# Accumulating transfers, PSUM sums and ScalarE block copies in a Mamba-and-FFN kernel

## The chip, the cores and the metric

The kernel runs on one core of one Trainium2 chip. The metric is the device time of one launch in microseconds (us), the median of three runs. TensorE is called PE, VectorE DVE, ScalarE ACT, GpSimd POOL; SyncE (SP) only issues transfers here.

## What is computed

The reference, cut to what matters: one row sequence of 4096 tokens with 1024 features goes through a selective-scan block and then through a linear layer with dequantised weights, both with a layer norm ahead and a residual behind.

```python
proj = layernorm(x) @ in_proj_w                       # 1024 -> 2 * 2048
x1, z = split(proj)
xc = silu(causal_conv(x1, width 4) + conv_b)          # per channel
ssm_p = xc @ x_proj_w.T                               # 2048 -> 64 + 16 + 16
dt_r, Bm, Cm = rmsnorm of the three parts of ssm_p
dt = softplus(dt_r @ dt_proj_w.T + dt_bias)           # 64 -> 2048
h_t = exp(dt_t * A) * h_(t-1) + dt_t * B_t * xc_t     # state: 2048 channels x 16
ys_t = sum over the 16 states of h_t * C_t
y = (ys + D * xc) * silu(z)
x = x + y @ out_proj_w.T                              # 2048 -> 1024
x = x + layernorm(x) @ W.T + bias                     # 1024 -> 1024, W dequantised
```

All of it is float32.

## The kernel before

**Chunks and steps.** The 4096 tokens are taken in 16 chunks of T = 256, the 2048 channels in 8 pairs of 128-channel tiles. The main part is 16 iterations (`c`) of 8 steps (`j`), 128 steps S = 8c + j, all written out. Step S does the scan of pair j of chunk c and, beside it, a piece of four other stages: the input projection of x for pair S + 9, of z and dt for S + 1, the small projection to dt, B and C (`pair_proj`) for S + 8, column block j of the out projection of chunk c - 1 (from c = 1 on) and column block j of the FFN of chunk c - 2 (from c = 2 on; its matmuls run at the start of the step after). "First" and "last" below are steps j = 0 and j = 7 of a chunk. They carry more: the first the transposes and ScalarE work of the second layer norm, the last those of the first layer norm and the root mean squares of dt, B and C. Nothing is scheduled by a tool: each engine runs its instructions in the order written, and semaphores hold it back.

**The scan.** A step has 16 units u of two states each, four units to a PSUM ring `hb0` to `hb3`. For a unit ACT saves the old state and writes two exponentials into the bank (`unit`, lines 1079 and 1083), DVE scans in place (line 1378) and multiplies by C into `hc` (`times_c`, line 1326); ACT may reuse a bank once the product of four units earlier is done. POOL makes the inputs `dbx` for two units at a time (`group_of_b`, line 486, 8 groups k of 4 states each a step, two buffers) and adds the halves of each group of `hc` into `half` (`group_sum`, line 494, 8 a step). PE adds each of these to `ys0` or `ys1` with two matmuls by the identity (`group_sum` of PE, line 574). After four groups DVE multiplies by the gate into `ybuf` (`y_gate`, line 1337): that of the second half stands in the next step, behind `product(1)` (`late_y`).

**Residual rows.** `x2` holds the rows of two chunks, 1 MB each, by parity of the chunk. Chunk c - 1 has its input loaded there in the first step of iteration c, and that buffer held chunk c - 3: so SP first waits for the last FFN block of c - 3, stores its rows to `out` (line 360), waits until that has landed, and loads the new rows (line 363). DVE adds an out-projection block from the PSUM bank `g1` onto these rows late in each step (`add_out`, behind `product(12)`), an FFN block early in the next (`add_ffn`, behind `product(0)`; both line 1304), and the small projection from `ys1` onto `ssm` (`pair_ss`, lines 1282 and 1285). POOL adds the bias to the rows in four parts a chunk (`add_bias`, line 504). `g1` is used by turns: FFN matmuls, DVE's add, out projection, DVE's add.

**Order on PE in a plain step** (neither first nor last): FFN block, late sums 6 and 7, half the out projection, `x_proj`, sum 0, half of x's input projection, sum 1, its other half, sums 2 and 3, dt, the other half of the out projection, half of z's, sum 4, the other half, sum 5.

## Time and profile before

| what | value |
|---|---|
| median of three runs | 4658.65 us (4651.46 to 4660.2) |
| the profiled execution, its own time | 4652.27 us |
| its span, first to last instruction | 4650.4 us |
| main part, 128 steps | from about 117 us to about 4515 us |
| a plain step from c = 2 on | 33.2 us |
| a whole chunk from c = 2 on | about 275.4 us |
| mean granted TensorE clock | 0.98 of full speed |

The profile is one execution, 1.9 us longer than its span, and 0.14% under the median. Busy shares of the four engines lie close together, so that the page's totals do not say who sets the pace: this is read from the stretches of single steps. One step is counted from one gate activation of ACT (line 1092) to the next, since this occurs once in a step.

### The profile page before, as it was taken

The page shows a single profiled execution, that of the slowest core. Times are in us where ns is not written, and L with a number is a line of the kernel's source. Part 1 is how long each engine was busy: PE and PEld are TensorE (multiplying, and loading weights), DVE is VectorE, ACT ScalarE, POOL GpSimd, SP SyncE. Part 2 cuts the span into 40 slices and gives each one's busy share as a digit, 9 for nine tenths or more (in the row PEclk, how much of TensorE's full clock was granted, in tenths as well). Part 3 has the DMA queues.
Part 4 walks back from the last instruction along what each step waited for, and adds up shares of the span by engine and source line. Part 5 has one row for each costly group of instructions (what it writes and reads, how often), then busy time and mean ns, then how long its engine had stood idle before and what let it go on. Part 6 is the DMA issues. An engine that isn't in the chain of part 4 may idle for free.

```text
span 4650.4 us, 80289 instructions
## 1 busy us (share of the span) xinstructions
PE 4425.4 (95%) x26656; PEld 4020.1 (86%) x26656; DVE 4164.3 (90%) x5745; ACT 3537.7 (76%) x8848; POOL 4034.5 (87%) x2942
## 2 busy tenths in 40 slices
PE   7788999999999999999999999999999999998879
PEld 6577889989898998989899898998989899897769
DVE  3899999999999999999999899999999999999871
ACT  3787787877878787787878878787887878777650
POOL 0898989989899998989899899999989999899870
PEclk9889999999999999999999999999999999999889
DMA  7324344353544435353444535335353443533232
GB/s 252 135 82 160 104 156 147 121 184 129 184 137 159 147 129 179 137 181 128 150 156 137 186 122 184 128 131 191 120 184 129 175 144 115 184 129 135 96 106 84
DMA packets 160286, 678.57 MB, mean 146 GB/s; under 512 B 21120, under 2 KB 30080, under 8 KB 110720
## 3 DMA queue, kind: packets, MB, share of 16 engines
q1 hardware_dynamic: 141440, 639.88, 39.6%
q10 hardware_dynamic: 18432, 33.56, 1.9%
q8 instruction: 212, 3.47, 0.3%
q14 instruction: 202, 1.65, 0.1%
HBM read 618.32 MB, written 55.05 MB: 145 GB/s over the span
## 4 chain that ended last, share of the span: by engine, by line
PE 65%; DVE 14%; POOL 8%; issue 7%; DMA 3%; ACT 2%; SPq 1%; POOLq 0%; DVEq 0%; ACTq 0%
PE gx L594 15%; PE ys L574 13%; PE g L767 12%; PE ys L614 12%; DVE hb L1378 9%; PE g L689 6%; POOL dbx L486 5%; DVE hc L1326 3%; POOL half L494 2%; PE ys L604 2%; PE ys L624 2%; PE hb L875 1%; DVE gx L1270 1%; DMA b_scratch<-ssmT 1%; DMA ybuf<-in_wf_scales 1%
## 5 line engine op out<-in xcount | busy, mean ns | idle before, releaser
L1378 DVE TENSOR_TENSOR_SCAN hb<-hb,dbx 128x512 f32<-128x512 f32 x2048 | 2496.7, 1219 | 110.8 <-ACT hb L1083 77.2
L486 POOL TENSOR_TENSOR dbx<-dtx,bb 128x1024 f32<-128x1024 f32 x1024 | 2421.2, 2364 | 68.9 <-DVE hb L1378 43.9
L1083 ACT ACTIVATE hb<-dt,a_neg 128x256 f32<-128x256 f32 x4096 | 1789.3, 468 | 66.3
L494 POOL TENSOR_TENSOR half<-hc 128x512 f32<-128x512 f32 x1024 | 1305.3, 1275 | 86.0 <-DVE hc L1326 85.1
L1326 DVE TENSOR_TENSOR hc<-hb,cb 128x512 f32<-128x512 f32 x2048 | 1376.2, 672 | 0.0
L574 PE MATMUL ys<-half,ident 128*128 128x256 f32 x4096 | 1057.2, 390 | 115.4 <-POOL half L494 99.1
L574 PEld LDWEIGHTS ys<-half,ident 128*128 128x128 f32 x4096 | 764.1, 194 | 242.9 <-POOL half L494 131.4
L767 PEld LDWEIGHTS g<-wo,ybuf 128*128 128x128 f32 x7680 | 909.3, 194 | 27.5 <-issue 15.2
L614 PE MATMUL ys<-xnT,wz 128*128 128x256 f32 x4096 | 931.5, 381 | 1.3 <-DVE ybuf L1337 1.3
L594 PE MATMUL gx<-xnT,wx 128*128 128x256 f32 x3968 | 903.6, 382 | 21.8 <-issue 11.0
L767 PE MATMUL g<-wo,ybuf 128*128 128x128 f32 x7680 | 915.0, 277 | 9.0 <-issue 9.0
L594 PEld LDWEIGHTS gx<-xnT,wx 128*128 128x128 f32 x3968 | 756.1, 191 | 131.5 <-issue 14.3
L614 PEld LDWEIGHTS ys<-xnT,wz 128*128 128x128 f32 x4096 | 773.2, 191 | 104.0 <-DVE ybuf L1337 2.1
L1079 ACT COPY hstate<-hb 128x2 f32<-128x2 f32 x2044 | 319.5, 156 | 703.2 <-DVE hc L1326 698.8
L689 PEld LDWEIGHTS g<-wf,x2nT 128*128 128x128 f32 x3552 | 414.1, 192 | 5.7
L689 PE MATMUL g<-wf,x2nT 128*128 128x128 f32 x3552 | 414.5, 275 | 0.0
L1270 DVE SCALAR_TENSOR_TENSOR gx<-xpre,convw,gx 128x256 f32<-128x256 f32 x744 | 301.9, 480 | 11.7 <-ACT gx L964 11.6
L1304 DVE TENSOR_TENSOR x<-g,x 128x256 f32<-128x256 f32 x240 | 99.8, 416 | 178.2 <-PE g L689 139.6
L512 POOL TENSOR_TENSOR dtx<-dt,xcs 128x2 f32<-128x2 f32 x128 | 25.3, 198 | 234.0 <-ACT dt L1014 227.8
L604 PE MATMUL ys<-xprojw,xcn 128*128 128x96 f32 x1024 | 140.7, 283 | 32.5 <-ACT xcn L973 23.8
L1089 ACT ACT_TABLE_LOAD x128 | 164.2, 1283 | 2.3
L1010 ACT ACT_TABLE_LOAD x128 | 164.2, 1283 | 2.3
(105 smaller groups left out, 2739.1 us busy)
## 6 DMA issues: line engine op xcount, KB each, us to landing
wz<-in_win SPq DMA_DIRECT2D x128, 1024.0 KB, 4.8
wx<-in_win SPq DMA_DIRECT2D x124, 1024.0 KB, 4.8
wo<-in_wout SPq DMA_DIRECT2D x123, 1024.0 KB, 5.0
wf<-wf_scratch SPq DMA_DIRECT2D x113, 512.0 KB, 3.9
xc_scratch<-xcn ACTq DMA_DIRECT2D x128, 256.0 KB, 3.7
xcs<-xc_scratch SPq DMA_DIRECT2D x128, 256.0 KB, 5.0
bb<-bc_scratch SPq DMA_DIRECT2D x64, 512.0 KB, 8.8
cb<-bc_scratch SPq DMA_DIRECT2D x64, 512.0 KB, 8.0
```

The source lines that it names most:

```text
L486: nc.gpsimd.tensor_tensor(dbx[:, k % 2, :].rearrange("p (n t) -> p n t", n=NQ), dtx[:, S % 2, a, :].unsqueeze(1).to_broadcast([P, NQ, T]), ...
L494: nc.gpsimd.tensor_tensor(half[:, k % 4, :], hc[:, k % 2, 0:HALF], hc[:, k % 2, HALF:GW], ALU.add).then_inc(halves, 1)
L574: mm = nc.tensor.matmul(ys[a][:, 0:T], ident[:], half[:, k % 4, i * T:(i + 1) * T], start=False, stop=(q == NQ - 1 and i == 1), skip_group ...
L594: mm = nc.tensor.matmul(pair_bank(q)[:, a * T:(a + 1) * T], pair_weights(q)[:, kk, a * P:(a + 1) * P], xnT[:, chunk % 2, kk, :], start=(kk ...
L614: mm = nc.tensor.matmul(ys[0][:, a * T:(a + 1) * T], wz[:, kk, a * P:(a + 1) * P], xnT[:, q // PAIRS % 2, kk, :], start=(kk == 0), stop=(k ...
L689: mm = nc.tensor.matmul(g1[:, tt * P:(tt + 1) * P], x2nT[:, kk, tt * P:(tt + 1) * P], wf[:, kk, :], start=(kk == 0), stop=(kk == KH - 1))
L767: mm = nc.tensor.matmul(g1[:, tt * P:(tt + 1) * P], ybuf[:, (1 - st.parity) * PAIRS + kt // 2, (kt % 2) * T + tt * P:(kt % 2) * T + (tt + ...
L1079: nc.scalar.copy(hstate[:, ds(2 * js * N + 2 * us, 2)], h[:, T - 1:UW:T]).then_inc(kept, 1)
L1083: ins = nc.scalar.activation(h[:, m * T:(m + 1) * T], dt[:, j % 2, a, :], ACT.Exp, scale=a_neg[:, ds((2 * j + a) * N + 2 * v + m, 1)])
L1270: nc.vector.scalar_tensor_tensor(bank[:, a * T:(a + 1) * T], xpre[:, a, tap:tap + T], convw[:, ds((2 * jq + a) * KC + tap, 1)], bank[:, a ...
L1326: nc.vector.tensor_tensor(hc[:, k % 2, w * UW:(w + 1) * UW], hb[u % 4][:], cb[:, n:n + 2, :].rearrange("p n t -> p (n t)"), ALU.mult).then ...
L1378: nc.vector.tensor_tensor_scan(h[:], h[:], dbx[:, k % 2, w * UW:(w + 1) * UW], 0.0, ALU.mult, ALU.add).then_inc(scans, 1)
```

## The change

- **Sums by a transfer.** Of the four groups of each half, the first two are now added by a transfer that POOL issues and that accumulates in SBUF (`add_group_pair`, 512 KB, twice a step); POOL adds the halves of the result (`pair_sum`). Six sums a step reach PE instead of eight, the order being groups 2 and 3 of the first half, its pair, group 2 of the second half, its pair, group 3. `half` has three places. PE's sums of the second half all move to the start of the next step.
- **Bias by a transfer.** One accumulating transfer of 1 MB a chunk instead of four POOL additions.
- **Blocks made onto their rows.** ACT copies a block of the rows into `g1` (`block_in`), PE's matmuls add onto it (`start=False`), and ACT copies it back (`block_out`). DVE's two adds a step are gone. ACT's copies stand behind unit 5 (FFN block out, out-projection block in) and at the step's end (out-projection block out, FFN block in).
- **dt, B and C** are summed over the eight pairs in the free columns of `g1`; ACT squares and copies the sum once a chunk and writes zeros. DVE's `pair_ss` is gone.
- **Order.** On PE `x_proj` and half of x's projection come ahead of the out projection, dt comes behind the first sum; on DVE `y_gate` of the first half comes two units later.
- SP's order of transfers is as before, but the store of the rows waits for `f_out`, which ACT's copy of the FFN block raises, where it waited for DVE's add.

The diff, cut to its core:

```diff
+        hd = sb("hd", [P, 3, GW])
         hc = sb("hc", [P, 2, GW])
-        half = sb("half", [P, 4, HALF])
+        half = sb("half", [P, PLACES, HALF])
...
                     if first and st.before(first).ffn:
-                        sp.wait_ge(f_add, after(PAIRS * (c - 2)))
+                        sp.wait_ge(f_out, after(PAIRS * (c - 2)))
                         sp.dma_start(out_rows[c - 3], x2_rows(1 - st.parity)).then_inc(out_st, 16)
...
+            def add_group_pair(S, a):
+                pool.wait_ge(hcs, after(UNITS * S + UNITS // 2 * a + 4))
+                pool.dma_start(hd[:, 2 * a, :], hd[:, 1, :], accum_op=ALU.add).then_inc(hd_acc, 16)
+            def pair_sum(S, a):
+                pool.wait_ge(hd_acc, 16 * (2 * S + a + 1))
+                nc.gpsimd.tensor_tensor(sum_place(SUMS * S + PAIR_SUM[a]), hd[:, 2 * a, 0:HALF],
+                                        hd[:, 2 * a, HALF:GW], ALU.add).then_inc(halves, 1)
...
+            def add_bias(chunk):
                 pool.wait_ge(l2_ready, after(2 * (chunk + 1)))
+                pool.dma_start(x2_rows(chunk % 2), ffn_bias.partition_broadcast(P).unsqueeze(1)
+                               .to_broadcast([P, TT, H]), accum_op=ALU.add).then_inc(bias_acc, 16)
...
+                    products(1)
+                    if not (first and c == 0):
+                        pair_sum(S - 1, 1)
+                        group_sum(S - 1, 1, 1)
+                    products(2)
+                    products(3)
+                    add_group_pair(S, 0)
+                    products(4)
+                    group_sum(S, 0, 0)
+                    products(5)
+                    group_sum(S, 0, 1)
+                    products(6)
+                    pair_sum(S, 0)
+                    if first and st.ffn:
+                        add_bias(c - 2)
+                    products(7)
+                    add_group_pair(S, 1)
...
             def pair_proj(q):
                 pe.wait_ge(sx_act, after(q + 1))
+                if q % PAIRS == 0:
+                    pe.wait_ge(ssm_zero, after(q // PAIRS + 1))
-                        mm = nc.tensor.matmul(ys[1][:, tt * E:(tt + 1) * E],
+                        mm = nc.tensor.matmul(g1[:, T + tt * E:T + (tt + 1) * E],
...
                     def ffn():
-                        if was.outproj:
-                            g1_after_o()
+                        pe.wait_ge(f_pre, after(S - 2 * PAIRS))
...
                     def out_proj(part):
-                            if was.ffn:
-                                g1_after_f()
+                            pe.wait_ge(o_pre, after(S - PAIRS + 1))
...
+                    def blocks_between():
+                        if st.inproj:
+                            act.wait_ge(xp_mm, after(S + PAIRS + 1))
+                        if st.before(first).ffn:
+                            ffn_out(S)
+                        if last and st.inproj:
+                            chunk_square(c + 1)
+                        if st.outproj:
+                            act.wait_ge(xres_in, landed(c))
+                            act.wait_ge(f_out, after(S - 2 * PAIRS))
+                            block_in(c - 1, j, o_pre)
+                    def out_out():
+                            act.wait_ge(o_mm, after(S - PAIRS + 1))
+                            block_out(c - 1, j, o_out)
+                    def ffn_in():
+                            act.wait_ge(o_out, after(S - PAIRS + 1))
+                            act.wait_ge(bias_acc, 16 * (c - 1))
+                            block_in(c - 2, j, f_pre)
...
                     unit(5)
                     norm1(1)
+                    blocks_between()
                     unit(6)
...
                     unit(15)
+                    if not last:
+                        out_out()
+                    ffn_in()
...
                     product(0)
-                    add_ffn()
...
                     product(4)
-                    add_x_proj()
...
                     product(12)
-                    add_out()
```

The order on PE from the start of a plain step, before. L689 is the FFN block, L574 a sum, L767 the out projection, L604 `x_proj`, L594 x's input projection.

```order
L689 MATMUL g<-wf,x2nT 128x128 [waits o_add,l2_evac,wf_in]
L689 MATMUL g<-wf,x2nT 128x128 x15
L574 MATMUL ys<-half,ident 128x256 [waits halves]
L574 MATMUL ys<-half,ident 128x256
L574 MATMUL ys<-half,ident 128x256 [waits halves]
L574 MATMUL ys<-half,ident 128x256
L767 MATMUL g<-wo,ybuf 128x128 [waits f_add,wo_in]
L767 MATMUL g<-wo,ybuf 128x128 x15
L604 MATMUL ys<-xprojw,xcn 128x96 [waits sx_act,y_ready]
L604 MATMUL ys<-xprojw,xcn 128x96 x3
```

The same place in the changed kernel (L721 FFN, L610 a sum, L642 `x_proj`, L630 x's projection, L794 the out projection).

```order
L610 MATMUL ys<-half,ident 128x256 [waits halves]
L610 MATMUL ys<-half,ident 128x256
L642 MATMUL g<-xprojw,xcn 128x96 [waits sx_act]
L642 MATMUL g<-xprojw,xcn 128x96 x3
L630 MATMUL gx<-xnT,wx 128x256 [waits sx_act,l1_evac,wx_in]
L630 MATMUL gx<-xnT,wx 128x256 x7
L794 MATMUL g<-wo,ybuf 128x128 [waits o_pre,wo_in]
L794 MATMUL g<-wo,ybuf 128x128 x7
```

The out projection now waits for ACT's copy (`o_pre`) with `x_proj` and half of x's projection ahead of it; in a first step x's projection is not ahead, so only `x_proj` is.

The order on ACT around unit 5 of a first step, before. L1079 and L1083 are a unit, L1102 the skip term, L931 a row of the second norm.

```order
L1102 ACTIVATE ys<-xcs,dparam 128x256 [waits xc_in0,sz_act]
L1079 COPY hstate<-hb 128x2 [waits hcs]
L1083 ACTIVATE hb<-dt,a_neg 128x256 [waits kept]
L1083 ACTIVATE hb<-dt,a_neg 128x256
L1079 COPY hstate<-hb 128x2 [waits hcs]
L1083 ACTIVATE hb<-dt,a_neg 128x256 [waits kept]
L1083 ACTIVATE hb<-dt,a_neg 128x256
L931 ACTIVATE xrow<-x,nmr,rstd 128x1024 [waits l1_tr]
```

And in the changed kernel (L1158 the skip term, L1135 and L1139 a unit, L1028 `block_out`, L1024 `block_in`).

```order
L1158 ACTIVATE ys<-xcs,dparam 128x256 [waits xc_in0,sz_act]
L1135 COPY hstate<-hb 128x2 [waits hcs]
L1139 ACTIVATE hb<-dt,a_neg 128x256 [waits kept]
L1139 ACTIVATE hb<-dt,a_neg 128x256
L1028 COPY x<-g 128x2x128 [waits f_mm,xp_mm]
L1024 COPY g<-x 128x256 [waits f_out,xres_in]
L1135 COPY hstate<-hb 128x2 [waits hcs]
L1139 ACTIVATE hb<-dt,a_neg 128x256 [waits kept]
L1139 ACTIVATE hb<-dt,a_neg 128x256
L954 ACTIVATE xrow<-x,nmr,rstd 128x1024 [waits l1_tr]
```

Two copies stand between units 5 and 6; the second waits for the loaded rows (`xres_in`).

The order on SP at the same place, in the changed kernel: the last transfer of a chunk and the next four.

```order
L409 DMA wz<-in_win 128x2048 [waits z_mm]
L372 DMA out<-x 128x2x1024 [waits f_out]
L375 DMA x<-in_x 128x2x1024 [waits out_st]
L380 DMA xcs<-xc_scratch 128x512 [waits dtx_ready,dx1]
L384 DMA wf<-wf_scratch 128x1024 [waits f_mm,wf_st]
```

No transfer moved; the store waits for `f_out`, the load for the store.

## Rows read from the trace of the kernel before

**Rows 1.** The page's engine totals: busy us, share of the span, instructions.

```profile
PE 4425.4 (95%) x26656; PEld 4020.1 (86%) x26656; DVE 4164.3 (90%) x5745; ACT 3537.7 (76%) x8848; POOL 4034.5 (87%) x2942
```

**Rows 2.** Stretches: length, busy of PE, PEld, DVE, ACT, POOL, granted clock, DMA, GB/s.

```profile
2217.20:2250.40 33.20, 33.20 (x206) 30.61 (x205) 32.33 (x46) 25.90 (x65) 30.81 (x23) 1.00 0.38 130
2322.00:2357.40 35.40, 33.29 (x200) 29.71 (x201) 31.12 (x42) 30.02 (x72) 33.53 (x27) 1.00 0.69 254
2283.40:2322.00 38.60, 36.96 (x230) 33.23 (x228) 34.67 (x51) 31.27 (x86) 31.29 (x24) 1.00 0.47 162
2046.70:2322.10 275.40, 270.70 (x1666) 247.89 (x1664) 259.06 (x359) 220.52 (x554) 251.99 (x183) 1.00 0.44 151
396.50:669.40 272.90, 251.97 (x1395) 224.20 (x1396) 256.84 (x352) 216.56 (x548) 247.63 (x181) 0.96 0.38 136
4243.00:4484.00 241.00, 201.93 (x1141) 176.44 (x1140) 205.42 (x254) 170.81 (x420) 219.28 (x159) 0.89 0.28 98
```

**Rows 3.** Chain that ended last, within one plain step: start us, us, what.

```profile
2217.39 1.73 PE ys L574 x8
2219.11 3.57 PE g L767 x32
2222.68 0.87 PE ys L604 x8
...
2224.44 3.45 PE gx L594 x16
```

**Rows 4.** DVE's groups in that plain step: busy us, mean ns, idle before.

```profile
L1304 DVE TENSOR_TENSOR x<-g,x 128x256 f32<-128x256 f32 x2 | 0.8, 416 | 1.0 <-PE g L689 1.0
...
L1285 DVE TENSOR_TENSOR ssm<-ys,ssm 128x192 f32<-128x192 f32 x1 | 0.3, 341 | 0.0
```

**Rows 5.** POOL's and ACT's groups by shape, over the whole span.

```profile
L486 POOL TENSOR_TENSOR dbx<-dtx,bb 128x1024 f32<-128x1024 f32 x1024 | 2421.2, 2364 | 68.9 <-DVE hb L1378 43.9 <-POOL bb L464 0.4
...
L494 POOL TENSOR_TENSOR half<-hc 128x512 f32<-128x512 f32 x1024 | 1305.3, 1275 | 86.0 <-DVE hc L1326 85.1
...
L1102 ACT ACTIVATE ys<-xcs,dparam 128x256 f32<-128x256 f32 x256 | 117.1, 457 | 0.0
```

**Rows 6.** Timeline of a plain step's start: start us, us, engine, instruction, idle before.

```profile
2212.98 1.22 DVE L1378 TENSOR_TENSOR_SCAN hb<-hb,dbx 128x512 f32<-128x512 f32 x1
...
2214.81 0.16 ACT L1079 COPY hstate<-hb 128x2 f32<-128x2 f32 x1 [0.65 <-DVE hc L1326]
...
2217.68 0.59 ACT L973 ACTIVATE xcn<-gx 128x512 f32<-128x512 f32 x1
...
2221.18 0.87 ACT L1083 ACTIVATE hb<-dt,a_neg 128x256 f32<-128x256 f32 x2
```

**Rows 7.** SP's timeline where a chunk ends: the store and the load.

```profile
2321.31 0.39 SPq L360 DMA_DIRECT2D out<-x  x1
2331.97 0.38 SPq L363 DMA_DIRECT2D x<-in_x  x1
```

**Rows 8.** Transfers by tile: times issued, KB each, median us to landing.

```profile
wf<-wf_scratch SPq DMA_DIRECT2D x113, 512.0 KB, 3.9
...
bb<-bc_scratch SPq DMA_DIRECT2D x64, 512.0 KB, 8.8
...
x<-in_x SPq DMA_DIRECT2D x16, 1024.0 KB, 5.0
out<-x SPq DMA_DIRECT2D x14, 1024.0 KB, 11.5
```

**Rows 9.** The store of line 360 alone, 13 of them.

```profile
DMA to landing us min/median/max: 6.5/11.5/11.9
```

**Rows 10.** Timeline in the last chunk: PE after it stood still.

```profile
4499.51 2.08 PE L574 MATMUL ys<-half,ident 128*128 128x256 f32 x4 [2.70 <-POOL half L494]
...
4504.91 5.29 PE L767 MATMUL g<-wo,ybuf 128*128 128x128 f32 x32
```

**Rows 11.** Issue of a transfer by SP where a queue is full: start us, us.

```profile
2332.45 1.84 SPq L368 DMA_DIRECT2D xcs<-xc_scratch  x1
```

More of the change, by code:

```diff
@@ L412, in store_columns @@
                 h = slice(half * H // 2, (half + 1) * H // 2)
-                sp.wait_ge(f_add, after(PAIRS * chunk + (half + 1) * PAIRS // 2))
+                sp.wait_ge(f_add, after(PAIRS * (chunk - NC + 2) + (half + 1) * PAIRS // 2))
                 sp.dma_start(out_rows[chunk][:, :, h], x2_rows(chunk % 2)[:, :, h]).then_inc(out_st, 16)
@@ L560, in _, with group_sum @@
             iterations(iteration)
-            group_sum(NC * PAIRS - 1, 7)
+            pair_sum(NC * PAIRS - 1, 1)
+            group_sum(NC * PAIRS - 1, 1, 1)
             for chunk in (NC - 2, NC - 1):
-                for i in range(4):
-                    add_bias(chunk, i)
+                add_bias(chunk)
         @block.tensor
         def _(pe):
-            def group_sum(SG, k):
-                a, q = divmod(k, NQ)
-                pe.wait_ge(halves, after(8 * SG + k + 1))
-                for i in range(2):
-                    mm = nc.tensor.matmul(ys[a][:, 0:T], ident[:], half[:, k % 4, i * T:(i + 1) * T],
-                                          start=False, stop=(q == NQ - 1 and i == 1), skip_group_check=True)
+            def group_sum(SG, i):
+                n = SUMS * SG + i
+                pe.wait_ge(halves, after(n + 1))
+                for w in range(2):
+                    mm = nc.tensor.matmul(ys[i // 3][:, 0:T], ident[:], half[:, n % PLACES, w * T:(w + 1) * T],
+                                          start=False, stop=(i % 3 == 2 and w == 1), skip_group_check=True)
                 mm.then_inc(sum_mm, 1)
@@ L634, in _ @@
             pe.wait_ge(id_ready, after(1))
+            for m in range(4):
+                mm = nc.tensor.matmul(g1[:, m * P:(m + 1) * P], ident[:], ident[:], start=(m == 0), stop=True,
+                                      skip_group_check=True)
+            mm.then_inc(g1_marked, 1)
             pe.wait_ge(l1_ready, after(2))
@@ L689, in ffn, with late_groups @@
                                 mm = nc.tensor.matmul(g1[:, tt * P:(tt + 1) * P], x2nT[:, kk, tt * P:(tt + 1) * P],
[L690 removed]
+                                                      wf[:, kk, :], start=False, stop=(kk == KH - 1),
+                                                      skip_group_check=True)
                         mm.then_inc(f_mm, 1)
[L693 removed]
+                    def late_groups():
                         if was.scan and not (first and c == 0):
[L695 removed]
+                            pe.wait_ge(dx1, after(S))
+                            for k in range(3, SUMS):
+                                group_sum(S - 1, k)
                     def group(k):
@@ L709, in x_proj @@
                         if st.inproj:
-                            if was.scan and not (first and c == 0):
-                                pe.wait_ge(y_ready, after(2 * S))
-                            else:
-                                pe.wait_ge(xp_add, after(S + PAIRS))
+                            if was.outproj and not was.ffn:
+                                pe.wait_ge(o_out, after(S - PAIRS))
                             pair_proj(S + PAIRS)
@@ L882, in _ @@
             pe.wait_ge(wf_in, landed(LAST - 2 * PAIRS))
-            pe.wait_ge(o_add, after(LAST - PAIRS))
+            pe.wait_ge(f_pre, after(LAST - 2 * PAIRS))
             for tt in range(TT):
@@ L886, in _ @@
                     mm = nc.tensor.matmul(g1[:, tt * P:(tt + 1) * P], x2nT[:, kk, tt * P:(tt + 1) * P],
-                                          wf[:, kk, :], start=(kk == 0), stop=(kk == KH - 1))
+                                          wf[:, kk, :], start=False, stop=(kk == KH - 1), skip_group_check=True)
             mm.then_inc(f_mm, 1)
-            group_sum(LAST - 1, 6)
+            pe.wait_ge(dx1, after(LAST))
+            for k in range(3, SUMS - 1):
+                group_sum(LAST - 1, k)
             pe.wait_ge(l2_ready, after(2 * (NC - 1)))
@@ L1465, in step @@
                     product(9)
-                    if not (last and st.norm1):
-                        y_gate(S, 0)
                     scan(11)
@@ L1471, in step @@
                     product(11)
-                    if last and st.norm1:
-                        y_gate(S, 0)
+                    y_gate(S, 0)
                     if not edge:
@@ L1493, in last_ffn @@
             def last_ffn(chunk, j):
-                dve.wait_ge(bias_add, after(4 * chunk + j // 2 + 1))
+                dve.wait_ge(bias_acc, 16 * (chunk + 1))
                 dve.wait_ge(f_mm, after(chunk * PAIRS + j + 1))
```

224 lines of the change are left out of this document (100 added, 124 removed).

## The prediction

> **What bounds the kernel now.** The page's totals come first: PE 95%, DVE 90%, POOL 87%, ACT 76% busy [rows 1]. They name no single bound, so the second view is the table by stretches. In a plain step of 33.2 us PE is busy for all of it, DVE for 32.33 us, POOL for 30.81, ACT for 25.9; over a whole chunk of 275.4 us PE is busy for 270.7 [rows 2]. The third view, the chain within such a step, holds nothing but PE's pieces one behind the other [rows 3]. So PE sets the pace from chunk 2 on, with DVE about 1 us a step behind it: its one idle time is the 1.0 us in which it waits for the FFN block [rows 4]. Where less falls to PE, in iteration c = 1 (no FFN), the chunk still takes 272.9 us with DVE at 256.84 [rows 2]: take PE away and DVE is next, at 94% of the time.
>
> **What PE loses.** Eight sums are 1.73 us a pair: 0.87 us each, two matmuls of two passes [rows 3]. Two go, so the plain step's PE work falls from 33.2 to 31.5 us, and the chunk's from 270.7 by 8 x 1.73 to 256.9.
>
> **What DVE loses.** Two adds of 0.416 us and one of 0.341 [rows 4], 1.17 us: 32.33 - 1.17 = 31.2 us of work. It is no longer held by the FFN block itself, but `late_y` still stands behind it, since all three sums of the second half come after that block.
>
> **What POOL loses and gets.** Two sums of 1.275 us a step [rows 5] and four bias additions a chunk of about the same go: 30.81 - 2.55 = 28.3 us or less. Two transfers a step come, plus one a chunk, and POOL is held while it issues them. No row shows POOL issuing a transfer. SP's issues take from 0.38 us [rows 7] to 1.84 us where a queue was full [rows 11], and POOL's longest instruction over the same 128x1024 tile takes 2.36 us [rows 5]. I take 1.3 us, near the middle, close to what POOL needs for half such a tile: 28.3 + 2.6 = 30.9 us, under PE's 31.5. From 1.6 us on POOL would set the pace, and at 2.36 us it would stand at 33.0, the step's length now.
>
> The Trainium skill (DMA: Bandwidth & Descriptors, SWDGE vs HWDGE vs iDMA and Latency and other measured facts) says that an accumulating transfer must come from GpSimd, whose cores write the descriptors, and puts the first byte at about 1 us; by that figure, an estimate, POOL's step would be 30.3 us, and nothing in the sum would move.
>
> **Landing.** The first transfer of a step is issued about 10 us after scan 0 and wanted by POOL about 20 us after it; the second is issued at about 24.5 and wanted at about 34.5. The window is some 9 us. Rows of 512 KB landed in 3.9 us (`wf`) and 8.8 us (`bb`, several at once) [rows 8]. An accumulating one also reads its target, so I take 6 us, hidden; the upper row just fits.
>
> **What ACT gets.** Four copies of 128x256 a step, priced by its skip term into PSUM, 0.457 us [rows 5]: 1.8 us. ACT was busy for 25.9 of 33.2 us, so there is room, but its copies are now in PE's chain. Let D be the start of scan 0 (2212.98). ACT starts unit 3 at D + 1.8, has the silu done at D + 5.3 and unit 5 at D + 9.1 [rows 6]; two copies later, at about D + 10.1, the rows are in `g1` (`o_pre`). PE meanwhile has the FFN block, three sums, `x_proj` and half of x's projection: about up to D + 10. From there to the end of the next step's late sums it has 27.1 us (4 x 1.79 out projection, 3 x 3.45 x and z, 6 x 0.87 sums, dt, FFN 3.57 [rows 3]), so `late_y` comes at D + 37.9 where DVE alone would reach it at D + 31.1 + 5.2 = D + 36.3. This asks PE and DVE to settle a little above 31.5; I take **31.9 us** for the plain step, 1.3 less than now.
>
> **The first step of a chunk, where the change costs.** Before, the last FFN block was added at the step's start, the rows stored at once (2321.31), the load issued 10.7 us later (2331.97) [rows 7], landed about 5.0 us after that [rows 8]; all this was hidden, because the loaded rows were wanted only by `add_out` behind `product(12)`, about 30 us into the step. Now the FFN block is copied out behind unit 5, and the very next instruction on ACT waits for the load that follows the store that follows this copy. Nothing covers it. In a first step ACT also has the start of the second norm (some 1.2 us), so the block is out at about D + 10.8. Store: 13 of them landed in 6.5 to 11.9 us, median 11.5 [rows 9], where they shared the engines with the chunk's B and C and z's weights (DMA share 0.69 [rows 2]). Now it starts 10 us later, when those have landed, so I take 6.5; load 5.0 [rows 8]; issue and copy 0.9. So `o_pre` comes at D + 23.2. Behind it on ACT's queue are all of units 6 to 15, so DVE and POOL stop too after a unit or two, and PE, which has only `x_proj` ahead of it in this step, stands from about D + 7.5, 15.7 us. After `o_pre` it has 7.2 out projection, 4 x 3.45 x and z, 6 x 0.87 sums, 0.87 dt, 1.8 transposes and 3.57 FFN, 32.4 us, up to the late sums of the next step: D + 55.6. In the settled loop these end 5.9 us into a step, so the next step begins at D + 49.7. PE that had stood still ran four passes in 2.08 us and the out projection's half in 5.29 where it takes 3.57 [rows 10, 3], with a granted clock of 0.89 in that chunk [rows 2]: 2 us more. **First step 52 us** in place of 35.4 [rows 2].
>
> The Trainium skill (DMA: Bandwidth & Descriptors, Anatomy of one DMA) gives a transfer 2.0 us plus its bytes over 436 GB/s, so an estimate of 4.4 us for 1 MB each way. The trace disagrees for both: 5.0 us for the load, never under 6.5 us for the store [rows 8, 9]. By the page the pair would take 8.8 us instead of 11.5, and the sum below would fall by 13 x 2.7 = 35 us.
>
> **The sum.** Last step: 38.6 us [rows 2], less 1.3 as the others, less 1.0 because dt now runs ahead of two sums: 36.3. A chunk: 52 + 36.3 + 6 x 31.9 = 279.7 us against 275.4, +4.3, times 12 for c = 3 to 14: +52. Iteration c = 2 has no store, so its first step is about 38.3 us and the chunk 266: -9.5. c = 1: DVE falls by 8 x 0.76 = 6.1 us of 256.84, and at the same share the chunk by 6.5. c = 0: -3. c = 15: PE is not its bound (201.93 of 241 us [rows 2]); 8 x 1.3 are saved, 12 lost to the store and load: +2. In the tail two transfers of 1 MB must land before the last FFN adds: +2. Together 52 - 9.5 - 6.5 - 3 + 2 + 2 = +37, say +40 to +45, since the waits I cannot see add time oftener than they take it. The profiled execution took 4652.3 us, 6 under the median: 4652 + 43 = 4695, and against the median about **4700 us**, 0.9% slower. The gain of some 1.3 us in 120 steps and a stall of 12 us and its aftermath in 13 steps nearly cancel.
>
> **Rivals.**
> 1. *The stall is shorter, faster than before.* If the rows are in `g1` 5 us earlier than I say in each first step (the store alone in 4 us, ACT early), 13 x 5 = 65 us go: 4635 us. For it: the store will be nearly alone. Against it: no store of 1 MB landed under 6.5 us. It becomes faster once store and load together take less than about 8 us. Chance 0.17 for under 4649.
> 2. *The store stays slow.* At the median of 11.5 us [rows 9] it adds 13 x 5 = 65 us: 4765. The first accumulating transfer of the step does start beside it. Chance 0.2.
> 3. *ACT's copies eat the gain.* If `o_pre` and `f_pre` hold PE so that the plain step stays at 33.2 us, about 100 steps lose 1.3 us: 4830. Chance 0.08.
> 4. *POOL's issue costs 2.4 us.* Then its step is 33.1 us of work and about 34.2 with its waits: 2.3 x 110 = 250 us more, 4950. Decides from 1.6 us. Chance 0.09.
> 5. *The accumulating transfer lands in 11 us*, over its window of 9: `pair_sum` holds POOL, the late sums and `late_y` by 2 us a step: 4900 or more. Chance 0.06.
>
> **How the numbers follow.** The forecast, 4650 to 4740, has 0.40. About 0.2% is what a measurement of this kernel can tell from no change, here 4649 to 4668: 0.1, from the forecast's lower end. Faster 0.17, slower 0.73. The range leaves out the lowest ends of rival 1 and rivals 4 and 5: 4625 to 4850.
>
> **What the profile after would show.** PE's sums 3072 passes instead of 4096; plain steps of about 31.9 us with PE still nearly full. In 13 first steps a wait of ACT of some 12 us on the load before a copy of `g1`, PE idle for 15 us before the out projection, SP's store and load issued back to back in the middle of the step's first half, and a lower granted clock behind it. POOL's issue near 1.3 us and no wait on `hd_acc`. The prediction is wrong if the wait for the rows is short, if plain steps are at 33 us or above, or if DVE waits for `dbx` in every step.

## The result: 3.1% slower

The changed kernel takes 4799.9 us (median of 4 runs, 4796.3 to 4805.0) against 4656.4 us beside it, a ratio of 1.031 with a 95% interval of 1.029 to 1.033: 143 us more, where some 43 were forecast. The sign and the stall in a chunk's first step were as forecast; the size was not, and most of what is missing lies in the last step of a chunk.

The page after, its totals and some of its costliest groups, answers to [rows 1, 4, 5]:

```profile
span 4803.2 us, 77941 instructions
...
PE 4304.4 (90%) x25640; PEld 3908.0 (81%) x25640; DVE 4054.7 (84%) x5385; ACT 3688.8 (77%) x9345; POOL 3887.9 (81%) x2894
...
L794 PE MATMUL g<-wo,ybuf 128*128 128x128 f32 x7680 | 1001.1, 288 | 207.5 <-ACT g L1024 207.5
...
L610 PE MATMUL ys<-half,ident 128*128 128x256 f32 x3072 | 808.4, 399 | 177.8 <-POOL half L516 103.7
...
L511 POOL DMA_DIRECT2D hd<-hd x256 | 225.8, 882 | 15.4 <-issue 2.9
L1024 ACT COPY g<-x 128x256 f32<-128x256 f32 x232 | 86.6, 373 | 164.1 <-DMA x<-in_x 139.3
```

PE, DVE and POOL have lost 121, 110 and 147 us of work, and the span has grown by 153. The 207.5 us that PE waits for ACT's copy of the rows (L1024, `block_in`) are the first thing to look at. The table by stretches (length, busy of PE, PEld, DVE, ACT, POOL, granted clock, DMA, GB/s) says where they lie: a plain step, the last step of a chunk, the first step and the second step of the next, and a whole chunk.

```profile
2500.90:2533.00 32.10, 31.69 (x197) 29.12 (x197) 31.11 (x42) 27.19 (x69) 30.04 (x23) 1.00 0.56 167
2629.80:2672.90 43.10, 36.76 (x214) 33.20 (x212) 32.62 (x47) 33.03 (x91) 28.68 (x23) 0.92 0.54 162
2672.90:2722.50 49.60, 36.17 (x208) 32.93 (x209) 31.90 (x41) 31.46 (x77) 33.60 (x27) 0.83 0.70 232
...
2672.90:2959.90 287.00, 264.93 (x1605) 242.25 (x1606) 252.54 (x336) 231.00 (x589) 244.41 (x182) 0.96 0.59 179
...
2722.50:2755.50 33.00, 32.55 (x202) 29.91 (x202) 31.18 (x42) 27.32 (x70) 30.11 (x23) 1.00 0.60 179
```

Steps are measured here and below from one silu of the gate to the next on ACT, as means over c = 3 to 13; the lines of a profile show single steps. The sum by steps:

| us | before | forecast | after |
|---|---|---|---|
| first step | 35.7 | 52 | 49.6 |
| second step | 34.9 | 31.9 | 33.0 |
| plain steps, five | 33.2 | 31.9 | 32.1 to 32.4 |
| last step | 38.5 | 36.3 | 43.1 |
| chunk | 275.2 | 279.7 | 287.0 |
| c = 2, first step | 36.5 | 38.3 | 44.5 |
| c = 2, chunk | 275.9 | 266 | 281.9 |

The forecast's chunk is 7.3 us too short, and the last step alone is 6.8 of it. The other errors (first -2.4, second +1.1, plain +1.8 in all) nearly cancel.

**The first step.** PE after the sums and `x_proj`; ACT; SP (start us, us, what, idle before):

```profile
2676.93 1.03 PE L642 MATMUL g<-xprojw,xcn 128*128 128x96 f32 x8
2689.75 7.45 PE L794 MATMUL g<-wo,ybuf 128*128 128x128 f32 x48 [11.79 <-ACT g L1024]
```
```profile
2678.00 0.37 ACT L1028 COPY x<-g 128x256 f32<-128x256 f32 x1 [0.21 <-PE g L642]
2689.23 0.38 ACT L1024 COPY g<-x 128x256 f32<-128x256 f32 x1 [10.86 <-DMA x<-in_x]
```
```profile
2678.40 0.39 SPq L372 DMA_DIRECT2D out<-x  x1
2683.89 0.38 SPq L375 DMA_DIRECT2D x<-in_x  x1
```

This is the forecast stall. The FFN block is out at 2678.37, the store is issued at 2678.40, the load 5.5 us later, and ACT goes on 5.3 us after that. PE stands for 11.8 us and then runs 48 passes of the out projection in 7.45 us, under a granted clock of 0.74 in that stretch and of 0.83 over the step. (A pass is what the trace counts: each float32 matmul of the kernel shows as two.) The Trainium skill (DMA: Bandwidth & Descriptors, Anatomy of one DMA) gives its 2.0 us plus bytes over 436 GB/s as a fit for transfers that GpSimd issues; taken for these two, which SP issues, it would make an estimate of 4.4 us each, and the trace has 5.5 and 5.3.

**The last step.** PE and ACT in the same stretch:

```profile
2632.14 0.60 PE L617 MATMUL gx<-ident,xrow 128*128 128x128 f32 x4
2634.22 0.66 PE L617 MATMUL gx<-ident,xrow 128*128 128x128 f32 x4 [1.48 <-ACT xnT L971]
2637.21 3.75 PE L794 MATMUL g<-wo,ybuf 128*128 128x128 f32 x16 [2.33 <-ACT g L1024]
2640.76 1.06 PE L617 MATMUL gx<-ident,xrow 128*128 128x128 f32 x4
```
```profile
2635.54 0.36 ACT L1028 COPY x<-g 128x256 f32<-128x256 f32 x1
...
2636.71 0.36 ACT L1024 COPY g<-x 128x256 f32<-128x256 f32 x1
...
2641.86 0.58 ACT L971 COPY xnT<-gx 128x512 f32<-128x512 f32 x1 [3.79 <-PE gx L617]
```

The norm transposes share one bank (`gx`), so between two of them PE waits for ACT's evacuation. Before, `x_proj` and a quarter of the out projection filled the first of these gaps. Now `x_proj` runs ahead of the transposes, and the out projection waits for `block_in`, which stands on ACT behind units 4 and 5, two evacuations and four small operations. PE stands for 1.5 and 2.3 us, runs the next 16 passes in 3.75 us at a granted clock of 0.50 (1.95 us where the clock is 1.00), and ACT, which wants the third transposes, waits 3.8 us for them. Which of these links carries the cost was settled only by experiment.

### The profile page after: what moved, and what is told of

Read it like the earlier page. It is cut to its first block, busy times and chain, and to the rows that moved or that the text cites. A ratio compares the mean times of both kernels' runs of the same rounds, so it can differ in the third digit from the quotient of the medians.

```text
span 4803.2 us, 77941 instructions
## 1 busy us (share of the span) xinstructions
PE 4304.4 (90%) x25640; PEld 3908.0 (81%) x25640; DVE 4054.7 (84%) x5385; ACT 3688.8 (77%) x9345; POOL 3887.9 (81%) x2894
## 3 DMA queue, kind: packets, MB, share of 16 engines
q1 hardware_dynamic: 141296, 639.35, 36.8%
## 4 chain that ended last, share of the span: by engine, by line
PE 48%; POOL 25%; issue 9%; DVE 8%; ACT 5%; DMA 5%; SPq 0%; POOLq 0%; ACTq 0%; DVEq 0%
POOL dbx L498 17%; PE ys L653 14%; PE ys L610 10%; PE g L794 9%; PE g L721 7%; DVE hb L1457 5%; PE gx L630 4%; POOL half L522 3%; POOL half L516 3%; ACT hb L1139 2%; POOL hd L511 2%; DMA x<-in_x 1%; DMA out<-x 1%; PE hb L896 1%; DVE gx L1353 1%
## 5 line engine op out<-in xcount | busy, mean ns | idle before, releaser
L1139 ACT ACTIVATE hb<-dt,a_neg 128x256 f32<-128x256 f32 x4096 | 1789.2, 468 | 66.4
L794 PE MATMUL g<-wo,ybuf 128*128 128x128 f32 x7680 | 1001.1, 288 | 207.5 <-ACT g L1024 207.5
L794 PEld LDWEIGHTS g<-wo,ybuf 128*128 128x128 f32 x7680 | 992.3, 204 | 236.9 <-issue 215.8
L610 PE MATMUL ys<-half,ident 128*128 128x256 f32 x3072 | 808.4, 399 | 177.8 <-POOL half L516 103.7
L630 PE MATMUL gx<-xnT,wx 128*128 128x256 f32 x3968 | 907.3, 382 | 23.3 <-issue 10.8
L653 PEld LDWEIGHTS ys<-xnT,wz 128*128 128x128 f32 x4096 | 779.6, 193 | 115.7 <-DVE ybuf L1421 11.8
L630 PEld LDWEIGHTS gx<-xnT,wx 128*128 128x128 f32 x3968 | 741.9, 192 | 123.1 <-issue 14.3
L610 PEld LDWEIGHTS ys<-half,ident 128*128 128x128 f32 x3072 | 572.1, 198 | 288.9 <-POOL half L516 134.6
L522 POOL TENSOR_TENSOR half<-hc 128x512 f32<-128x512 f32 x512 | 650.6, 1271 | 175.3 <-DVE hc L1410 175.0
L1410 DVE TENSOR_TENSOR hd<-hb,cb 128x512 f32<-128x512 f32 x1024 | 688.8, 673 | 0.0
L1410 DVE TENSOR_TENSOR hc<-hb,cb 128x512 f32<-128x512 f32 x1024 | 688.8, 673 | 0.0
L1135 ACT COPY hstate<-hb 128x2 f32<-128x2 f32 x2044 | 318.6, 156 | 476.7 <-DVE hc L1410 393.7
L721 PEld LDWEIGHTS g<-wf,x2nT 128*128 128x128 f32 x3552 | 414.1, 192 | 5.7
L721 PE MATMUL g<-wf,x2nT 128*128 128x128 f32 x3552 | 414.5, 275 | 0.0
L516 POOL TENSOR_TENSOR half<-hd 128x512 f32<-128x512 f32 x256 | 325.5, 1272 | 0.9 <-DMA hd<-hd 0.9
L1421 DVE TENSOR_TENSOR ybuf<-ys,gate 128x256 f32<-128x256 f32 x256 | 107.4, 420 | 235.7 <-PE ys L610 235.5
L511 POOL DMA_DIRECT2D hd<-hd x256 | 225.8, 882 | 15.4 <-issue 2.9
L1024 ACT COPY g<-x 128x256 f32<-128x256 f32 x232 | 86.6, 373 | 164.1 <-DMA x<-in_x 139.3
```

The lines of the kernel that those rows point to most:

```text
L516: nc.gpsimd.tensor_tensor(sum_place(SUMS * S + PAIR_SUM[a]), hd[:, 2 * a, 0:HALF], hd[:, 2 * a, HALF:GW], ALU.add).then_inc(halves, 1)
L522: nc.gpsimd.tensor_tensor(sum_place(SUMS * S + LATER_SUMS[a][i]), hc[:, i, 0:HALF], hc[:, i, HALF:GW], ALU.add).then_inc(halves, 1)
L610: mm = nc.tensor.matmul(ys[i // 3][:, 0:T], ident[:], half[:, n % PLACES, w * T:(w + 1) * T], start=False, stop=(i % 3 == 2 and w == 1), s ...
L630: mm = nc.tensor.matmul(pair_bank(q)[:, a * T:(a + 1) * T], pair_weights(q)[:, kk, a * P:(a + 1) * P], xnT[:, chunk % 2, kk, :], start=(kk ...
L653: mm = nc.tensor.matmul(ys[0][:, a * T:(a + 1) * T], wz[:, kk, a * P:(a + 1) * P], xnT[:, q // PAIRS % 2, kk, :], start=(kk == 0), stop=(k ...
L721: mm = nc.tensor.matmul(g1[:, tt * P:(tt + 1) * P], x2nT[:, kk, tt * P:(tt + 1) * P], wf[:, kk, :], start=False, stop=(kk == KH - 1), skip ...
```

## Experiments

**1. The order of transposes and out projection on PE.** First theory: ACT's wait for the transposes.

```
 # last step
 norm1(0); norm1(1)
+norm1(2)
 out_proj(0)
-norm1(2)
 out_proj(1)
 # first step
 out_proj(0); out_proj(1)
-out_proj(2); norm2(0); out_proj(3); norm2(1)
+norm2(0); out_proj(2); norm2(1); out_proj(3)
```

> The changed kernel with another order on TensorE in two places and nothing else: in a chunk's last step the third group of norm transposes stands ahead of out_proj's first quarter (it stood behind it), and in a chunk's first step the norm transposes stand after the second and third quarter of out_proj instead of after the third and fourth. Theory A: the last step lost because ScalarE waits 3.0 + 0.9 us there for transposes that queue behind an out_proj that itself waits for ScalarE's block_in, and the first step because the transposes stand behind 24 matmuls of out_proj at half clock (3.3 us). Then the last step falls from 43.2 to about 39.3 us, the first step by about 3 us (c=2 from 44.5 to 41.5), and the time by 15 x 3.9 + 14 x 3 = about 100 us, to 4700. Rival B: the last step is long because ScalarE has 2 to 3 us more work of its own in it (block copies, the copy of the sums, zeroing); the order changes nothing and the last step stays at 43, the time at 4795 to 4805.

Measured: 4793.4 us, 1.030 (1.029 to 1.032); last step 42.5, first 49.7. Nearly nothing. But the trace of its last step shows that the order only exchanged one wait for another: the fourth transposes now stand behind 32 passes that take 6.4 us.

```profile
ACT xnT L971 <- PE gx L617: 4.6, 1, 4.6
```

So for the last step this run did not decide; in the first step the transposes came 16 passes sooner and the step did not move, so they were not its bound.

**2. Store and load of the rows in halves**, columns 0 to 511 a few steps ahead.

```
-if first: wait f_out(last block of c-3); store rows c-3; wait; load rows c-1
+if first:  wait f_out(last block of c-3); store columns 512.. of c-3
+if j == 1: wait that store;               load  columns 512.. of c-1
+if j == 5: wait f_out(block 3 of c-2);    store columns ..511 of c-2
+if j == 6: wait that store;               load  columns ..511 of c
```

> The changed kernel with the store of the finished rows and the load of the next x rows into the same buffer cut into column halves: columns 0 to 511 are stored in step 5 of the chunk before and loaded in step 6, so that only columns 512 to 1023 move after the last ffn block is out, and out_proj's first block waits for neither. Theory A: the first step of c=3 to 15 is long because block_in waits for store and load in series (10.2 us on ScalarE, 13.4 us on TensorE), but part of that only hides other waits, which c=2's first step (44.5 us, no store in it) shows: 49.4 falls to 44.5, times 13 is 64 us, time 4736. Rival B: the stall is paid in full and nothing else is long there: 49.4 falls by 13.4 to 36, the first step of before, times 13 is 174 us, time 4626. Rival C: the moved transfers hold SyncE's queue in steps 5 and 6 (6.5 us store ahead of the load), later weights come late, and steps 5 to 7 take back 3 to 6 us a chunk: 4790 or more.

Measured: 4637.8 us, 0.9976 (0.9965 to 0.9987): 162 us less than the changed kernel. First steps fall from 49.6 to 38.0 us, and that of c = 2 from 44.5 to 37.5, so rival B came near (11.6 of 13.4 us a step) and theory A fell: c = 2 was no picture of a first step without the stall. It has no store, but its load is issued directly behind the B, C and z loads and takes 12.4 us, from 668.86 to the copy at 681.22, in the changed kernel:

```profile
668.38 0.43 SPq L409 DMA_DIRECT2D wz<-in_win  x1
668.86 0.43 SPq L375 DMA_DIRECT2D x<-in_x  x1
```
```profile
681.22 0.38 ACT L1024 COPY g<-x 128x256 f32<-128x256 f32 x1 [5.90 <-issue]
```

The trace of before has a like spread for its load (line 363, 15 of them):

```profile
DMA to landing us min/median/max: 4.8/5.0/12.6
```

The two long ones, 12.2 and 12.6 us, are those of c = 1 and c = 2, the chunks without a store; all others took 4.8 to 5.4.

The moved transfers cost nothing visible (rival C): plain and last steps stay at 32.1 to 32.4 and 42.7 us. The last step is hardly touched by it (43.1 to 42.7), so it is a loss of its own.

**3. The sums and the bias alone**, on the kernel before; blocks and `x_proj` sums stay with DVE. The places of PE's sums, of dt and of `y_gate` move with the sums, as in the change.

```
+hd[0..2]; add_group_pair (accumulating transfer), pair_sum, six sums a step
+add_bias by one accumulating transfer
 add_ffn(); add_out(); add_x_proj()   # as before, on DVE
```

> The kernel before with only two parts of the change: the first two groups of each half are added by an accumulating transfer (six sums on GpSimd and TensorE instead of eight), and the bias is added by one accumulating transfer. The out_proj and ffn blocks and the x_proj sums stay with VectorE's additions as before, in their old places, so there is no block_in and no stall behind the rows' store and load. Theory A: what the plain step won (33.2 to 32.2 us) is GpSimd's four sums less; it comes here too, first and last step stay as before (36 and 38.5 us), and the time is 4656 - 15 x (5 to 7 steps x 1.0 us) = 4550 to 4580. Rival B: it is VectorE's relief of three additions a step (VectorE is busy 94% of a chunk before), so the plain step stays at 33.2 and the time at 4645 to 4670. Rival C: transfer landing 5.6 us late delays the pair sum so that y_gate waits; with VectorE's additions behind it the step is longer than before: 4700 or more.

Measured: 4553.5 us, 0.979 (0.978 to 0.981). Theory A came true, and the kernel is faster than the one before and the changed one. The same stretches as above (plain, last, first, chunk):

```profile
2379.80:2412.10 32.30, 31.89 (x198) 29.12 (x197) 32.14 (x45) 26.00 (x66) 30.13 (x23) 1.00 0.56 165
2509.00:2545.70 36.70, 33.96 (x214) 30.33 (x212) 34.15 (x50) 31.21 (x86) 29.62 (x24) 1.00 0.62 185
2545.70:2581.50 35.80, 33.48 (x208) 29.85 (x209) 30.73 (x42) 29.99 (x71) 32.54 (x26) 1.00 0.99 325
2545.70:2813.30 267.60, 260.18 (x1603) 236.26 (x1604) 258.49 (x359) 220.17 (x554) 242.84 (x181) 1.00 0.63 192
```

The plain step is 32.3 us with DVE's three additions still in it, and on the mean of the five plain steps hardly less without (32.34 and 32.27): taking them from DVE is worth 0.1 us, the sums by transfer 0.9. How much of the 0.9 is PE's work, POOL's or the new places is not separated. The clock stays at 1.00.

**4. The complement**: the changed kernel with eight sums on POOL and PE.

```
-add_group_pair, pair_sum, six sums
+group_sum(S, 0..7), in before's places
```

> The complement: the changed kernel with the eight group sums on GpSimd and TensorE as before; blocks made onto their rows and left to ScalarE, the x_proj sums in PSUM and the bias transfer stay. Theory A (the win of the plain step is GpSimd's): the plain step goes back to 33.2 or more, a chunk to 286.8 + 6 to 8 us, the time to 4890 to 4920. Rival B (the win is VectorE's relief): plain step 32.2, time 4790 to 4810, as the changed kernel.

Measured: 4927.5 us, 1.060 (1.058 to 1.061). Plain step 33.5, chunk 296.7 (9.7 more than the changed kernel's), last step 43.8, first 49.8. So the blocks on ACT bring the long first and last steps by themselves, and win nothing in between. Only in c = 15, where PE has no in-projection, is it other: from its second step on its steps take 31.1 to 31.4 us here, 33.1 to 34.8 in the changed kernel, 32.1 to 36.1 before. There the blocks on ACT did shorten the step, and the transfers lengthened it beside them; without the blocks they did not (31.3 to 33.7 in run 3). Why is open.

**5, 6. All four transposes ahead of the out projection**, with the rows in halves; and with `out_out` behind unit 15.

```
 norm1(0); norm1(1)
+norm1(2); norm1(3)
 out_proj(0); out_proj(1)
 # and in 6, on ACT
-if last: out_out()      # ahead of unit(14)
 unit(14); x_taps(); unit(15)
-if not last: out_out()
+out_out()
```

> The split-rows kernel (4637.8 us; last step 43.2 us) with TensorE's order in a chunk's last step changed: all four groups of norm transposes stand ahead of out_proj's first quarter. The norms-first kernel had only exchanged the third group for a wait of 4.6 us for the fourth, behind 32 matmuls of out_proj (6.4 us at half clock), so it decided nothing. Theory A (ScalarE is held by transposes that queue behind out_proj): ScalarE's wait falls to under 1.5 us, the last step from 43.2 to 39.5, times 14 is 50 us, time 4588. Rival B (ScalarE's own added work, and VectorE and TensorE waiting for it, is what lengthens the step): out_proj starts 2 to 3 us later instead, the step stays at 42 to 43.5, time 4620 to 4645.

> As norms4_split, and in the last step the out_proj block is copied back after ScalarE's unit 15, as in all other steps, not between second_skip_term and unit 14, where ScalarE stands 1.5 us for out_proj's last quarter. Theory A: that wait is on the path of the exps that VectorE waits for: the last step is another 1.5 us shorter than norms4_split's, 14 x 1.5 = 21 us. Rival B: the copy is then late for the next ffn block, TensorE waits at the start of the next chunk, and the time is that of norms4_split or up to 15 us more.

Measured: 4629.1 us, 0.994 (0.993 to 0.996), last step 42.4; and 4634.4 us, 0.996 (0.994 to 0.997), last step 42.3. Theory A falls, this time cleanly: ACT's wait for the fourth transposes is down to 0.24 us and the step has not moved. PE has taken the wait over (4.1 us for evacuations), and ACT waits later, for the dt projection:

```profile
2547.95 1.11 PE L632 MATMUL gx<-ident,xrow 128*128 128x128 f32 x4 [1.83 <-ACT xnT L986]
```
```profile
2549.10 0.59 ACT L986 COPY xnT<-gx 128x512 f32<-128x512 f32 x1 [0.24 <-PE gx L632]
...
2562.72 0.17 ACT L1082 ACTIVATE dt<-ys 128x2 f32<-128x2 f32 x1 [2.45 <-PE ys L678]
```

What both orders leave as it was is that PE has nothing to run in the gaps. That gave the theory of run 9.

**7. The bias alone**, on the kernel before.

```
-add_bias(c - 2, 0..3): four additions on POOL
+add_bias(c - 2): one accumulating transfer
```

> The kernel before with only the bias changed: one accumulating transfer of 1 MB a chunk in the first step instead of four additions of 1.27 us on GpSimd. Theory A: GpSimd is not the bound of a plain step before (30.7 of 33.2 us, TensorE 33.2 of 33.2), the additions were hidden, so what the sums-and-bias kernel won (96 us) is all the sums': 4640 to 4655 here. Rival B: the transfer, landing after some 10 us beside the first step's loads, delays those: first step 36 to 38, time 4660 to 4680. Rival C: the bias additions held the step: 4600 to 4635.

Measured: 4656.9 us, 1.000 (0.999 to 1.001); chunk 275.3. No difference, so the 96 us that run 3 won beside its own runs of before come with the sums.

**8. The second transfer of a step issued 5.8 us later**, behind the small operations and the next step's first products, on run 3's kernel.

```
 products(7)
-add_group_pair(S, 1)
 inflow_of(S + 1); carry_of(S + 1); group_of_b(S + 1, 0, ...)
+add_group_pair(S, 1)
```

> The sums-and-bias kernel (4553.5 us) with the second accumulating transfer of a step issued after GpSimd's small operations (inflow, carry, the next step's first products) and not ahead of them. Theory A: the small operations are long (inflow 0.52 us for 0.24, carried 0.50 for 0.26, dtx 1.59 for 1.27) because the issue of the transfer is still going on behind them; issued later they go back to their times of before. In a plain step TensorE is busy 31.9 of 32.3 us, so the time hardly moves: 4540 to 4555. Rival B: those durations stay, they belong to another neighbour (VectorE's or the transfers' traffic); and the pair sum, 4 us later, comes too late for the late groups: 4560 to 4590.

Measured: 4751.9 us, 1.021 (1.019 to 1.022): 198 us more than run 3. Half of theory A holds: the small operations are back at 0.29 (inflow), 0.30 (carried) and 1.32 us (dtx), and the sum now behind the issue is long in some steps (median 1.31 us, up to 1.62, for 1.27). Its forecast of the time failed, and rival B's was far too low: POOL waits 124 times for the landing, in all 172.5 us; in run 3 that wait was 0.3 us in all, in the changed kernel 0.9.

```profile
L507 POOL TENSOR_TENSOR half<-hd 128x512 f32<-128x512 f32 x256 | 325.1, 1270 | 173.0 <-DMA hd<-hd 172.5
```

The issue in a plain step of run 3, from the products ahead of it to the pair's sum (L507):

```profile
2397.33 2.37 POOL L489 TENSOR_TENSOR dbx<-dtx,bb 128x1024 f32<-128x1024 f32 x1
2399.64 0.81 POOL L502 DMA_DIRECT2D hd<-hd  x1
...
2409.82 1.27 POOL L507 TENSOR_TENSOR half<-hd 128x512 f32<-128x512 f32 x1
```

And in run 8:

```profile
2515.14 2.37 POOL L489 TENSOR_TENSOR dbx<-dtx,bb 128x1024 f32<-128x1024 f32 x1
2517.46 0.21 POOL L528 TENSOR_TENSOR dtx<-dt,xcs 128x2 f32<-128x2 f32 x1
2517.61 1.27 POOL L532 TENSOR_TENSOR dtx<-dt,xcs 128x510 f32<-128x510 f32 x1
2518.84 0.24 POOL L542 TENSOR_TENSOR inflow<-dtx,b 128x32 f32<-128x32 f32 x1
...
2523.23 0.89 POOL L502 DMA_DIRECT2D hd<-hd  x1
...
2528.30 1.27 POOL L507 TENSOR_TENSOR half<-hd 128x512 f32<-128x512 f32 x1 [0.55 <-DMA hd<-hd]
```

From issue to sum POOL had 10.2 us, now 4.5 and the wait; the transfer took 5.0.

Plain steps grow by 0.7 us only, first steps from 36.3 to 43.6: there the landing is late beside the B and C loads. The waits of one such step (in all, times, longest):

```profile
DVE ybuf L1369 <- PE ys L601: 9.0, 2, 7.5
...
PE ys L601 <- POOL half L507: 6.6, 1, 6.6
...
POOL half L507 <- DMA hd<-hd: 4.2, 1, 4.2
```

**9, 10. ACT's block copies early in the last step**, with the rows in halves and with the changed kernel's own store and load.

```
 silus()
+if last: blocks_between()
 unit(4); first_skip_term(); norm1(0); unit(5); norm1(1)
-blocks_between()
+if not last: blocks_between()
 # PE, last step
 norm1(0)
+out_proj(0)
 norm1(1)
-out_proj(0)
 norm1(2); out_proj(1); norm1(3)
```

> The split-rows kernel (4637.8 us, last step 43.2 us) with ScalarE's block copies and the copy and zeroing of the sums put directly behind the silus in a chunk's last step (they stood behind unit 5 and the second norm evacuation), and on TensorE out_proj's first quarter directly behind the first norm transposes, as before the change. Theory A, formed after the two order kernels failed: TensorE has nothing to do between the norm transposes because out_proj is held by block_in until ScalarE has done units 4 and 5 and two evacuations; it stands 4.6 us there (1.5 + 0.8 + 2.3) and then runs at half clock, which makes 32 out_proj matmuls 6.4 us instead of 3.7. With block_in some 3 us earlier out_proj fills those gaps: granted clock of the last step from 0.92 to 0.98 or more, last step from 43.2 to 37.5 to 38.5, times 14 is 70 us, time 4560 to 4575. Rival B: ScalarE is simply short of time in this step (33 of 43 us busy, in pieces that VectorE waits for); units 4 and 5 come 1.6 us later now, VectorE waits for them, and the step stays at 42 to 43: 4625 to 4640.

> The changed kernel with ScalarE's block copies early in a chunk's last step as in blocks_early_split, but with the rows' store and load whole and in series as the change has them. If the two losses are separate, each is worth the same alone as beside the other: blocks_early_split was 50 us under split_rows, so this is 4800 - 50 = 4750, and the two together (162 + 50 us under the changed kernel's 4800) make the 4588 measured. If the stall at the chunk's start hides what the last step loses (the transfers' start depends on a block that ScalarE copies in the first step, so everything before it shifts alike), no such hiding is expected; were it there, the time would be 4790 to 4805.

Measured: 4587.6 us, 0.986 (0.984 to 0.987), last step 39.0; and 4754.6 us, 1.021 (1.020 to 1.023), last step 39.2. The last step of run 9, and PE at its start:

```profile
2521.80:2560.80 39.00, 34.08 (x214) 30.67 (x212) 33.20 (x47) 33.03 (x93) 29.34 (x23) 1.00 0.60 179
```
```profile
2524.19 0.60 PE L632 MATMUL gx<-ident,xrow 128*128 128x128 f32 x4
2526.07 2.02 PE L809 MATMUL g<-wo,ybuf 128*128 128x128 f32 x16 [1.28 <-ACT g L1039]
2527.93 0.61 PE L632 MATMUL gx<-ident,xrow 128*128 128x128 f32 x4
2529.37 0.66 PE L632 MATMUL gx<-ident,xrow 128*128 128x128 f32 x4 [0.82 <-ACT xnT L986]
```

The same matmuls and the same copies; PE's waits ahead of the third transposes are one of 1.3 us and one of 0.8 in place of 1.5 and 2.3, the 16 passes take 2.02 us, not 3.75, PE's busy time falls from 36.7 to 34.1 us and the granted clock rises from 0.92 to 1.00. Theory A holds as a mechanism, though the step (39.0 us) and the time (4588) stop short of its ranges, 37.5 to 38.5 and 4560 to 4575. The edit moves ACT's copies and PE's quarter together; runs 1 and 5 had moved PE's order alone to little effect (0.6 and 0.3 us off the last step). Rival B falls for these 3.7 us: ACT is busy for 33.0 us as before, and the step is shorter. The two losses nearly add: run 2 gave back 162 us, run 10 gave back 45, both together 212.

## Why the prediction was right, and where it was wrong

- **Plain step, 33.2 to 31.9: nearly.** 32.3 us. PE, not ACT's copies, bounds it (31.69 busy of 32.10), so rival 3 did not come true, and run 3 shows that DVE's relief, weighed as a gain in the text, is worth only 0.1 us of it. One sum in the working is off: D + 10.1 and 27.1 us make D + 37.2, not D + 37.9, and nothing accounts for the 0.7 us.
- **POOL's issue, 1.3 us: high.** 0.88 us for each of 256; rival 4 did not come true. The forecast missed that what waits for the operations behind an issue comes 0.2 us later.
- **Landing, 6 us in a window of 9: held,** 5.6 us median, POOL waited once. In the medians the first transfer of a step landed in 4.6 us of a window of 10.6, the second in 6.8 of 9.6. In first steps the second took 10.9, as rival 5 had it, but there its window was 12.8. Issuing the second 5.8 us later cost 198 us (run 8).
- **First step, 52 us: held,** 49.6, in its parts too: ACT waited 139.3 us for the load in 13 steps, 10.7 each, for the 12 forecast. PE stood for 11.8 us ahead of the out projection, not 15.7, since it had waited 2.6 us for late sums before. The store took 5.5 us, not the 6.5 that was the least before, the load 5.3 for 5.0. Run 2, by taking the chain away, won 11.6 us a step.
- **c = 2, "no store, so about 38.3 us": failed.** 44.5. The load had been given the median landing of 5.0 us [rows 8]; issued directly behind the B, C and z loads it took 12.3. This could have been read before the run: the load of c = 2 had taken 12.6 us in the trace of before, hidden behind a median of 15 [rows 8].
- **Last step, "38.6 less 1.3 less 1.0: 36.3": the step that failed.** 43.1, and 6.8 us too little in each of the twelve chunks c = 2 to 13 is some 82 of the missing 100 us. The term took PE's and dt's savings and left out what `block_in` does there, although the text had just put ACT's copies into PE's chain. In a plain step PE has FFN, sums, `x_proj` and half of x's projection to run until the rows are in `g1`. In the last step x's projection cannot start before four transposes have passed through one bank, and each waits for ACT. The out projection was what filled those gaps. By letting it do so again, runs 9 and 10 took 3.7 and 3.9 us from the step (42.7 to 39.0 and 43.1 to 39.2), of the 6.8 that the term was short. The rest of the term was sound: with the sums alone (run 3) the last step takes 36.8 us.
- **The ends, which no run takes up.** c = 0 and 1 together were forecast 9.5 us shorter and came out 0.2 longer; c = 15 was to be 2 longer and was 8.5 longer up to its last step; what follows was to be 2 longer and was 2.7 shorter. The last step of c = 14, without transposes or an x projection, grew too (33.8 to 37.4 us, with 3.6 us of PE's wait for `block_in`); run 4 has 4.2 us of that wait there and takes 33.4, so the wait alone does not explain that one.
- **Chance and range.** The time lies in the upper part of the range, but by a way that no rival names: rival 2 (4765) asked for a slow store, which did not come. That it lies in the range is luck.

What remains in the last step, 39.0 us in run 9 against 36.8 in run 3, stays open. Two differences are on record, and no run parts them. ACT is busy 1.8 us longer in run 9's (33.0 for 31.2), and DVE waits 4.0 us there for ACT's exponentials, a wait that run 3's last step does not have; and `x_proj` is not back in the gap between the transposes.

## What to carry to other kernels

Ask of each step kind apart what its engine has to run while a newly added wait is open. A wait that is hidden in the plain step because other work lies ahead of it is bare in the one step where that work depends on the same waited-for engine. And a part of a change that takes work from an engine that isn't the bound should be tried apart from the part that shortens the bound: here the second alone is 2.1% faster, both together 3.1% slower, and with both losses mended (run 9) they stand at 4588 us against its 4554.

## What the runs showed of the hardware

- A wait cost PE twice here. After waits of 1.5 and 2.3 us, with one piece of 0.66 us between them, it ran 16 passes of 128x128 in 3.75 us at a granted clock of 0.50 (1.2 of 2.4 GHz); after one of 1.3 us (run 9) in 2.02 at 1.00; where it had not stood they take 1.95. After 11.8 us of standing the granted clock was 0.50 for another 3.9 us, and 0.83 over the step.
- POOL goes on before the issue of an accumulating transfer is over, and what stands behind it ends later. In the changed kernel:

```profile
2521.18 0.83 POOL L511 DMA_DIRECT2D hd<-hd  x1
2521.79 0.46 POOL L537 TENSOR_TENSOR dtx<-dt,xcs 128x2 f32<-128x2 f32 x1
2521.94 1.52 POOL L541 TENSOR_TENSOR dtx<-dt,xcs 128x510 f32<-128x510 f32 x1
2523.17 0.49 POOL L551 TENSOR_TENSOR inflow<-dtx,b 128x32 f32<-128x32 f32 x1
```

  The next operation starts 0.61 us after the issue has, which is shown until 0.83. Each of the next few is shown 0.25 us longer than in run 8, where they stand ahead of the issue, but they start behind each other as there: 0.15 and 1.23 us apart in both. Only what waits for the last of them is later, 0.72 us behind its start for 0.48, so that the delay is some 0.2 us once and not for each. Why is open; only their place was shown to matter. The Trainium skill (Perfetto Trace Analysis, DMA Instruction — SWDGE (GPSIMD)) says that the end shown is the end of descriptor writing and not of the transfer; the trace agrees, 0.88 us shown and 5.6 us to landing.
- Landing depends on what was issued just ahead: 1 MB of x rows took 5.3 us behind nothing, 12.3 us behind the B, C and z loads; 1 MB of rows stored took 5.3 us in the median in the changed kernel, where it starts late, and 11.7 in run 3, where it starts beside them.

```profile
out<-x SPq DMA_DIRECT2D x14, 1024.0 KB, 5.3
```
